# Decoder layer on one Trainium2 core: three hand-written step orders rearranged, the weight loads of the first batch issued one pair earlier, and two small gate operations moved from GpSimd to VectorE

## What is computed

```python
x = x + attention(layernorm(x), w_qkv, w_out)      # causal, 16 heads of 64
x = x + cross(layernorm(x), ctx, Wq, bq, Wk, bk)   # softmax((ctx Wq')(ctx Wk')') mixes the 1024 columns
x = x + ffn(layernorm(x))                          # 8 experts, one chosen per row
# ffn: cont = (select_weight . (x - mean)/|x - mean|)**2 ; score = cont.sum()
#      gate = sigmoid(slope*(score - center)); best expert e, scale s = gate[e]
#      out = (1-s)*x + s*(bias[e] + degen[e] (update[e]' (x - debias[e])))
```

## Time and profile before

| | |
|---|---|
| runs | 2547.31, 2555.49, 2560.07 us; median 2555.49 |
| the profiled execution | 2547.31 us; its span from the first to the last instruction is 2545.5 us |
| busy share of the span | PE 93%, DVE 70%, ACT 32%, POOL 28% |
| mean granted TensorE clock | 0.979 of full speed |
| DMA | 393.49 MB, mean 155 GB/s |

### The profile page before, as it was taken

One profiled execution on the slowest core, in us unless ns is written; L12 is line 12 of the kernel. 1 busy time (PEld: TensorE's weight loads), 2 busy tenths in 40 slices (PEclk: granted clock), 3 DMA queues, 4 the chain that ended last, 5 costly groups with the idle time before them and its releaser, 6 DMA issues.

```text
span 2545.5 us, 38106 instructions
## 1 busy us (share of the span) xinstructions
PE 2367.7 (93%) x14435; PEld 1165.9 (46%) x14435; DVE 1787.2 (70%) x3393; ACT 821.0 (32%) x1629; POOL 721.3 (28%) x1045
## 2 busy tenths in 40 slices
PE   4888889899999999999999999989999999999997
PEld 1333434454544444454454444445454444445444
DVE  6676778756967677766876676775695777776566
ACT  2444333412223433431213333442222434342120
POOL 3232343224312222213522222222431222222231
PEclk9999999899999999999999999999999999999997
DMA  7688888976747867886845778787673677687543
GB/s 215 168 186 170 180 184 180 243 161 140 150 107 145 157 138 144 165 207 145 161 109 128 150 146 157 147 210 158 139 149 105 143 158 146 139 170 184 116 77 106
DMA packets 983130, 393.49 MB, mean 155 GB/s; under 512 B 936796, under 2 KB 946012, under 8 KB 982948
## 3 DMA queue, kind: packets, MB, share of 16 engines
q1 hardware_dynamic: 977908, 372.72, 68.5%
q10 hardware_dynamic: 5040, 18.35, 2.5%
HBM read 122.56 MB, written 33.55 MB: 61 GB/s over the span
## 4 chain that ended last, share of the span: by engine, by line
PE 64%; DVE 19%; DMA 7%; issue 4%; ACT 3%; POOL 2%; SPq 1%; ACTq 0%; DVEq 0%; POOLq 0%
PE ps_p L591 10%; PE ps_p L593 10%; PE ps_p L592 10%; PE ps_s L651 6%; PE ps_s L591 6%; PE ps_s L593 6%; PE ps_s L592 6%; PE ps_o L679 6%; DMA r<-pn 5%; DVE pn L931 3%; DVE bn L936 2%; DVE peak L971 2%; DVE vn L1203 2%; PE ps_s L656 2%; ACT probs L834 1%
## 5 line engine op out<-in xcount | busy, mean ns | idle before, releaser
L1224 POOL TENSOR_SCALAR pn<-probs,rden 128x640 f16<-128x640 f32 (+7 forms) x512 | 390.6, 777 | 1194.0 <-DVE rden L983 678.5
L834 ACT ACTIVATE probs<-ps_s,low,sizes 128x640 f32<-128x640 f32 (+7 forms) x512 | 421.7, 827 | 761.6 <-DVE low L974 645.7
L931 DVE SCALAR_TENSOR_TENSOR pn<-probs,rden,pn 128x640 f16<-128x640 f32 (+7 forms) x512 | 444.1, 904 | 144.8 <-POOL pn L1224 143.3
L591 PE MATMUL ps_p<-r,w 128*128 128x512 f16 x1344 | 511.1, 380 | 0.8 <-DVE r L1215 0.6
L592 PE MATMUL ps_p<-r,w 128*128 128x512 f16 x1344 | 510.9, 380 | 0.0
L593 PE MATMUL ps_p<-r,w 128*128 128x512 f16 x1344 | 510.6, 380 | 0.0
L971 DVE TENSOR_REDUCE peak<-ps_s 128x2 f32<-128x1280 f32 (+3 forms) x128 | 241.5, 1886 | 95.0 <-PE ps_s L656 93.8
L651 PE MATMUL ps_s<-qk 64*128 64x512 f16 (+3 forms) x2304 | 234.5, 328 | 50.9 <-ACT probs L834 44.2
L679 PE MATMUL ps_o<-r,vn 128*64 128x512 f16 (+3 forms) x2208 | 209.5, 347 | 40.5 <-issue 40.2
L593 PEld LDWEIGHTS ps_p<-r,w 128*128 128x128 f16 x1344 | 131.8, 98 | 159.8 <-issue 2.1
L591 PE MATMUL ps_s<-r,pn 128*128 128x512 f16 x512 | 194.3, 379 | 9.2 <-DMA pn<-pn 9.2
(11 more groups left out here) (191 smaller groups left out, 3523.5 us busy)
## 6 DMA issues: line engine op xcount, KB each, us to landing
w<-w_pairs SPq DMA_DIRECT2D x72, 512.0 KB, 4.1
r<-wo_pairs SPq DMA_DIRECT2D x16, 1024.0 KB, 6.1
w_raw<-in_x SPq DMA_DIRECT2D x32, 512.0 KB, 4.3
out<-r SPq DMA_DIRECT2D x32, 512.0 KB, 2.9
w_pairs<-w SPq DMA_DIRECT2D x24, 512.0 KB, 4.3
qk<-in_x SPq DMA_DIRECT2D x24, 512.0 KB, 4.5
w_raw<-in_ctx_t SPq DMA_DIRECT2D x16, 512.0 KB, 5.6
late<-in_w_out ACTq DMA_DIRECT2D x13, 512.0 KB, 4.0
```

The lines of the kernel that those rows point to most:

```text
L591: pe.matmul(ps, lh, rh, start=start and k == ks[0], stop=False)
L834: act.activation(probs_part(q, j, w), ps_s[:, j, scores(q)], ACT.Exp, bias=low[:, n % 2, i:i + 1], scale=sc(n), accum_out=den[:, n % 2, i: ...
L931: dve.scalar_tensor_tensor(out=to, in0=bank, scalar=scale, in1=rounded, op0=ALU.mult, op1=ALU.subtract).then_inc(ok, 1)
L1224: pool.tensor_scalar(to, src, scale, 1.0, ALU.mult, ALU.mult).then_inc(ok, 1)
```

## The change

It does five things.

1. In `PE_BODY`, `S7` moves ahead of `P200+`.
2. In batch 0 the loads `WI0` and `WI1` go out at the end of ACT's body, one pair earlier (`+++`), instead of behind `E11`; the first two are issued at the end of `ACT_START`. `WN0++` and `WN1++` move forward in the body.
3. In the tail DVE's `KL` and `JL0` move from ahead of `L10` and `L20` to behind `R3`; `QH1`/`QL1` go ahead of `JH2`/`JL2` on ACT and DVE, `R5` and `RA0` move behind others, and `QL3` ahead of `RA0`.
4. In `PE_TAIL`, `G3` moves ahead of `B01`.
5. The inverse norm moves from POOL's `TS` to DVE's `GA`: two operations of one column, each with a wait for itself.

The renumbering of the later gate steps is left out here.

```diff
-    P111+ P112+ P113+ P200+ S7 P201+ P202+ P203+ P210+ P211+ S0+ S1+ P212+ P213+
+    P111+ P112+ P113+ S7 P200+ P201+ P202+ P203+ P210+ P211+ S0+ S1+ P212+ P213+
-    E00 E01 CH21 E10 E11 WI0++ WI1++ E20 E21 WI2++ CH00+ E30 E31 OH1- WN0++ E40 E41 CH01+ WN1++ E50 E51 CH10+ WN2++ OH0
-    E60 E61 CH11+ E70 E71 CH20+
+    E00 E01 CH21 E10 E11 WN0++ E20 E21 WI2++ CH00+ WN1++ E30 E31 OH1- E40 E41 CH01+ E50 E51 CH10+ WN2++ OH0 E60 E61
+    CH11+ E70 E71 CH20+ WI0+++ WI1+++
...
-    S2 S3 M1- S4 G0 S5 G1 M0 S6 G2 B00 S7 B01 G3 B10 B11 M1 B20 N0 B21 N1 B30 N2 B31 N3 B40 N4 B41 N5 B50 N6 B51 N7
+    S2 S3 M1- S4 G0 S5 G1 M0 S6 G2 B00 S7 G3 B01 B10 B11 M1 B20 N0 B21 N1 B30 N2 B31 N3 B40 N4 B41 N5 B50 N6 B51 N7
-    L70- L71- X1 CL21 R0 L00 L01 X2 R1 X3 KL L10 L11 R2 JL0 L20 L21 R3 OL1- X4 L30 L31 R4 QL0 JL1 X5 L40
-    L41 R5 JL2 QL1 OL0 X6 L50 L51 R6 QL2 JL3 X7 L60 L61 R7 RA0 L70 L71 QL3 RA1 LB0 OL1 CX0 LL0 LB1 CR0 RA2 CX1 CLO0
+    L70- L71- X1 CL21 R0 L00 L01 X2 R1 X3 L10 L11 R2 L20 L21 R3 KL JL0 OL1- X4 L30 L31 R4 QL0 JL1 X5 L40
+    L41 QL1 JL2 R5 OL0 X6 L50 L51 R6 QL2 JL3 X7 L60 L61 R7 QL3 RA0 L70 L71 RA1 LB0 OL1 CX0 LL0 LB1 CR0 RA2 CX1 CLO0
...
-    E00 E01 CH21 E10 E11 E20 E21 KH JH0 E30 E31 OH1- E40 E41 QH0 JH1 E50 E51 JH2 QH1 OH0 E60 E61 QH2 JH3 E70 E71
+    E00 E01 CH21 E10 E11 E20 E21 KH JH0 E30 E31 OH1- E40 E41 QH0 JH1 E50 E51 QH1 JH2 OH0 E60 E61 QH2 JH3 E70 E71
...
-    AX0+ AX1+ AX2+ WN0+ AX3+ WN1+ AX4+ WN2+ AX5+ AX6+ AX7+ CH00+ CH10+ CH20+ CH01+ WN0++ WN1++ CH11+ WN2++ CH21+
+    AX0+ AX1+ AX2+ WN0+ AX3+ WN1+ AX4+ WN2+ AX5+ AX6+ AX7+ CH00+ CH10+ CH20+ CH01+ WN0++ WN1++ CH11+ WN2++ CH21+ WI0+++ WI1+++
...
                     gate_step(dve.scalar_tensor_tensor(out=sel_u[:, :], in0=ps[:, 0:64], scalar=c_ffn, in1=ffn_c[:, 0:64],
                                                        op0=ALU.mult, op1=ALU.subtract), T, 1)
                     dve.tensor_tensor(sel_sq[:, :], sel_u[:, :], sel_u[:, :], ALU.mult)
+                    gate_step(dve.tensor_scalar(g1[:, 0:1], mv3[:, i, 1:2], float(DM) / UP_X ** 2, rs3[:, i:i + 1], ALU.mult,
+                                                ALU.mult), T, 2)
+                    gate_step(dve.tensor_scalar(g1[:, 1:2], g1[:, 0:1], rs3[:, i:i + 1], None, ALU.mult), T, 3)
+                    dve.tensor_reduce(g8[:, 0, :], sel_sq[:, :].rearrange("p (n s) -> p n s", s=SEL), AX_X, ALU.add)
                     gate_step(dve.scalar_tensor_tensor(out=g8[:, 1, :], in0=ps[:, 128:FW], scalar=c_ffn2,
-                                                       in1=ffn_c[:, 128:FW], op0=ALU.mult, op1=ALU.add), T, 2)
-                    dve.tensor_reduce(g8[:, 0, :], sel_sq[:, :].rearrange("p (n s) -> p n s", s=SEL), AX_X, ALU.add)
-                    dve.wait_ge(d_inv, T + 1)
-                    gate_step(dve.tensor_scalar(g8[:, 2, :], g8[:, 1, :], ve3[:, i:i + 1], None, ALU.add), T, 3)
-                    gate_step(dve.reciprocal(g8[:, 1, :], g8[:, 2, :]), T, 4)
-                    gate_step(dve.tensor_tensor(g8[:, 3, :], g8[:, 0, :], g8[:, 1, :], ALU.mult), T, 5)
-                    gate_step(dve.tensor_tensor(g8[:, 2, :], g8[:, 3, :], center_b[:, :], ALU.subtract), T, 6)
+                                                       in1=ffn_c[:, 128:FW], op0=ALU.mult, op1=ALU.add), T, 4)
+                    gate_step(dve.tensor_scalar(g8[:, 2, :], g8[:, 1, :], g1[:, 1:2], None, ALU.add), T, 5)
+                    gate_step(dve.reciprocal(g8[:, 1, :], g8[:, 2, :]), T, 6)
+                    gate_step(dve.tensor_tensor(g8[:, 3, :], g8[:, 0, :], g8[:, 1, :], ALU.mult), T, 7)
+                    gate_step(dve.tensor_tensor(g8[:, 2, :], g8[:, 3, :], center_b[:, :], ALU.subtract), T, 8)
                     dve.tensor_tensor(g8[:, 4, :], g8[:, 2, :], slope_b[:, :], ALU.mult).then_inc(f_z, 1)
                     dve.scalar_tensor_tensor(out=low_h[:, i % 2, 0:64], in0=ps[:, 64:128], scalar=c_ffn, in1=ffn_c[:, 64:128],
                                              op0=ALU.mult, op1=ALU.subtract).then_inc(f_read, 1)
 
...
                         rounded(xh2[:, 0, :], xn2, 1.0, b_hi)
                     elif kind == "TS":
                         sigma(T, mv3[:, i, :], ve3[:, i:i + 1], rs3[:, i:i + 1], sh3[:, i:i + 1], d_mv, d_ve, d_rs, d_sh)
-                        pool.tensor_scalar(ve3[:, i:i + 1], mv3[:, i, 1:2], rs3[:, i:i + 1], float(DM) / UP_X ** 2,
-                                           ALU.mult, ALU.mult).then_inc(d_step, 1)
-                        pool.wait_ge(d_step, T + 1)
-                        pool.tensor_scalar(ve3[:, i:i + 1], ve3[:, i:i + 1], rs3[:, i:i + 1], 1.0,
-                                           ALU.mult, ALU.mult).then_inc(d_inv, 1)
                     elif kind == "TH":
                         pool.wait_ge(d_xn, T + 1)
                         if T > 0:
```

More of the change, by code:

```diff
@@ L289, in decoder_layer @@
         b_bn, b_mv, b_ve, b_rs, b_sh, b_xn, b_hi, b_lo, t2_in = sems("b_bn b_mv b_ve b_rs b_sh b_xn b_hi b_lo t2_in")
-        d_step, d_inv = sems("d_step d_inv")
         d_bn, d_mv, d_ve, d_rs, d_sh, d_xn, d_hi, d_lo, t3_in = sems("d_bn d_mv d_ve d_rs d_sh d_xn d_hi d_lo t3_in")
@@ L1073, in ffn_rest @@
                                              in1=ffn16[:, 0, :, :], op0=ALU.mult, op1=ALU.subtract)
-                STEPS = 11
+                STEPS = 13
                 def gate_step(ins, T, count):
@@ L1100, in gate_choice @@
                     dve.wait_ge(f_e, T + 1)
-                    gate_step(dve.tensor_scalar(g8[:, 6, :], g8[:, 5, :], 1.0, None, ALU.add), T, 7)
-                    gate_step(dve.reciprocal(g8[:, 7, :], g8[:, 6, :]), T, 8)
-                    gate_step(dve.tensor_reduce(g1[:, 2:3], g8[:, 7, :], AX_X, ALU.max), T, 9)
+                    gate_step(dve.tensor_scalar(g8[:, 6, :], g8[:, 5, :], 1.0, None, ALU.add), T, 9)
+                    gate_step(dve.reciprocal(g8[:, 7, :], g8[:, 6, :]), T, 10)
+                    gate_step(dve.tensor_reduce(g1[:, 2:3], g8[:, 7, :], AX_X, ALU.max), T, 11)
                     dve.tensor_scalar(g1[:, 4:5], g1[:, 2:3], -1.0 / UP_X, 1.0 / UP_X, ALU.mult, ALU.add)
                     gate_step(dve.scalar_tensor_tensor(out=g8[:, 8, :], in0=g8[:, 7, :], scalar=g1[:, 2:3], in1=rank[:, :],
-                                                       op0=ALU.is_equal, op1=ALU.mult), T, 10)
-                    gate_step(dve.tensor_reduce(g1[:, 3:4], g8[:, 8, :], AX_X, ALU.max), T, 11)
+                                                       op0=ALU.is_equal, op1=ALU.mult), T, 12)
+                    gate_step(dve.tensor_reduce(g1[:, 3:4], g8[:, 8, :], AX_X, ALU.max), T, 13)
                     dve.tensor_scalar(low_h[:, i % 2, 64:GK], g8[:, 8, :], g1[:, 3:4], g1[:, 2:3], ALU.is_equal,
```

## The result

The changed kernel takes 2568.89 us, the median of the first five runs, from 2564.62 to 2572.17. The kernel before takes 2555.49. The ratio is worked out over all 28 runs of the changed kernel, whose median is 2572.7: it is 1.0067, 95% interval 1.0052 to 1.0084, slower by 0.67%, or 17 us. The profiled execution has a span of 2569.5 us. I take it in the order of the prediction's steps.

A forecast was written before the change was run, and what follows sets the result against it. PE was taken as the bound, busy 45.60 of 46.00 us in a batch 1 pair, DVE in the tails' ffn part. Terms 16 - 22 + 2 + 12 + 7 = +15 us on 2555.5 gave 2570.5; range 2554 to 2593.

The forecast's parts named there:

- S7: +16 forecast: Body pairs: S7 ahead of P200 waits 0.82 us for its input in 21 pairs and pair 6 of batch 0; +16 us.
- What could shrink are PE's short waits for E: Body pairs of batches 1 to 3: PE's short waits, some 10 us at most, give 2 us back.
- Loads and start: -20 forecast: Batch 0: earlier weight loads shorten pairs 1 to 5, -22 us; the start comes later, +2.
- The M1- of pairs 1 to 5 should then look like that of pair 6: Batch 0: with loads gone from T7's flight, pairs 1 to 5 approach pair 6's 50.57 us; at best 27.1 gained.
- Rival (a): Batch 0: early loads make T6 late instead, M1- still waits; loads give 0 to -8, sum +29 to +37; chance 0.20.
- its own counter-argument: Batch 0, against a late T6 costing time: L10 waits for T7's landing anyway, and pair 6's H00 to L10 fits ahead.
- The forecast's weaker case: Batch 0: T6 is hurt as much as T7 was, 3.8 us, and about half the loads' gain is lost: -12 us.
- Tails: +12 forecast: Four tails: moved DVE and ACT steps and G3 ahead of B01 delay G0, G2 and M1; +3 us each.
- T7 lands some 3 us later than before, M1 with it: Each tail: RA0 waits for B01's end, so L70, L71 and T7 come later and M1 waits; +3 us.
- the upper bound: Each tail: the pauses drop PE to the half clock again; +5 us a tail.
- Gate: +7 forecast: GA on DVE: two more steps cost 0.40 us each GA, 2.0 in three tails and 0.8 at the end.
- DVE is without slack from GA0 to XB7: The ffn part of each tail: DVE sets the time, so five longer GA delay XB7 by 2.0 us in three tails.

The follow-up runs named there:

- E00: A step of ACT in the kernel, not a follow-up run; in the new order the load WI1 stands ahead of it in pair 0.
- E31: A step of ACT in the kernel, not a follow-up run; PE's S4 waits for it.
- E61: A step of ACT in the kernel, not a follow-up run; PE's S7 needs it.

## Why the prediction was right

The sum was right, its terms were not. Forecast +15, measured +17; one by one:

- **S7: +16 forecast, +11 measured.** The wait is 0.80 for a forecast 0.82, in the very 21 pairs. It stands in pair 6 of batch 0 too, as forecast. The step that was mis-sized is "What could shrink are PE's short waits for E ... I take 2 back": 3 to 8 came back, of the 10 the prediction named as the most. S4's wait for E31 is slack that sits behind the new pause, early in the next pair.
- **Loads and start: -20 forecast, -9 measured.** The mechanism held where it could act: -4.6 a pair in pairs 3 to 5, for a forecast -4.4. "The M1- of pairs 1 to 5 should then look like that of pair 6" failed for pairs 1 and 2, since pair 6 is free of the scan's loads as well, not only of WI. With those out of the way the five pairs gave 20.9 of the 22. The start: S2 of pair 0 began at 84.08 for a forecast 84.0, but it cost 3.9 at S4 in place of 2, so S3 and S4 took nothing of it up. Rival (a), that T6 becomes the victim, was right in its premise (6.1 to 10.9) and wrong in its price: L10 waits for T7 anyway, as its own counter-argument said. The Trainium skill ("DMA: Bandwidth & Descriptors", section on queues, rings and completion order) speaks of turns packet by packet, and the trace agrees that whatever transpose is in flight pays, T6 and T7 alike. The forecast's weaker case, -12 for the loads and -10 with the start, comes near to the -9 measured, but by luck: it is pairs 1 and 2 that lack, and not a half of every pair by a late T6. What decides the time is which transpose somebody waits for. What one more load beside it costs is not shown: in the kernel before, T7 took 11.4 us ahead of pair 1, where four loads of 512 KB left during its flight, and 10.7 ahead of pair 4, where three did.
- **Tails: +12 forecast, +17 measured by themselves.** In the whole change the four tails are 13.2 us longer from S3 to M1, so this term was nearly right there. The waits of G0 (1.7 forecast, 3.15, 2.88, 1.25 and 0.40 in the four tails) and G2 (2 forecast, 1.74) came. "T7 lands some 3 us later than before, M1 with it" was wrong in its path: M1 waits in none of the tails. What RA0 and JL3 delay first is B10 and G3, and there the swap costs 2.6 us a tail, twice the 1.3 that the forecast's 3 leaves for it beside the 1.7 of G0 and G2. The clock, which the prediction kept only for the upper bound, is the other part: in the tail's own run seven more stretches of G0 to G2 are below 0.7, and in the one shown G2 costs 4.41 - 2.94 = 1.5 us more. Which stretches drop differs from tail to tail and from kernel to kernel; why is not shown.
- **Gate: +7 forecast, 0 measured.** "DVE is without slack from GA0 to XB7" was the failed step. The row it rested on the earlier trace rows shows the slack: four waits of WLO, 3.4 us, each right behind a GA. What WLO waits for does depend on GA, by way of GE on ACT, but ACT came to GE later than GA's result did, being busy with TX. So 0.49 us more cost nothing, and 1.23 us cost 0.63.

The parts measured alone sum to 11 - 9 + 0 + 17 = +19, the whole gives +17 (13 to 21). Set beside the parts, the forecast had two terms too high, by 12 in all (S7, gate), and two too low, by 16 (loads, tails), which cancelled to within 4 us. The forecast was right by its signs and its largest waits, and by luck in the sum.

## What to carry to other kernels

A table of waits that looks small must be read by place. Here a wait right behind the lengthened step took up 0.49 us whole, since the chain over other engines that it waited for had started beside the step and was longer; at 1.23 us the step was the longer chain and the rest was paid. A wait behind a new pause took up part of it. If a good stretch is taken as the model for a bad one, list everything that leaves in each, all queues, before the difference is put down to one transfer: here two groups of loads each kept T7 late in pairs 1 and 2, and only the move of both freed it (-23 us against -9 and +5). A swap of two equal blocks on the bounding engine is not free when one of them then comes ahead of its input or its bank; here it cost 2.6 us a tail.

## What the hardware showed that I had not expected

After pauses of 0.8 us in an otherwise full TensorE the granted clock stayed at 1.00 in all 21 cases; after 2.1 us it fell in 5 of 21, and in the tails, where several pauses of 1.7 to 3 us follow one another, it was under 0.7 in 5 to 10 of 12 stretches, against 3 in the kernel before. A small DVE step, 128 x 8 elements, took 1.04 us in place of 0.17 when it began just behind a POOL operation of 1.05 us. The Trainium skill ("SBUF — State Buffer", section on who interferes with whom) describes the port pair shared by these two engines as an exclusive lock, held for a whole instruction, and counts among the cases a VectorE instruction with two inputs in SBUF beside a GpSimd instruction that reads SBUF; the trace agrees, 1.04 against 1.05.
